# Attention with a quantised feed-forward layer on one core: SyncE's transfers by need, the exponential ahead of the rounding, the last rstd earlier

## What is computed

```python
def _L0_xattn_ref(q1, key, value, weights, bias, drop_mask):
    scores = jnp.einsum('bqd,bkd->bqk', q1, key) / 0.72
    attn = jax.nn.softmax(scores, axis=-1) * drop_mask
    o = jnp.einsum('bqk,bkd->bqd', attn, value) + bias
    return jnp.einsum('bqd,de->bqe', o, weights)

def _L0_ffn_ref(x, weight_q, weight_scale, bias):
    amax = jnp.max(jnp.abs(x2d), axis=-1, keepdims=True)
    x_scale = jnp.maximum(amax, EPS) / 127.0
    x_q = jnp.clip(jnp.round(x2d / x_scale), -128, 127).astype(jnp.int8)
    acc = jax.lax.dot_general(x_q, weight_q, (((1,), (1,)), ((), ())), preferred_element_type=jnp.int32)
    return acc.astype(jnp.float32) * x_scale * weight_scale[None, :]  (+ bias)

x = x + _L0_xattn_ref(_layernorm(x), ctx, ctx, weights, bias, mask)
x = x + _L0_ffn_ref(_layernorm(x), weight_q, weight_scale, ffn_bias)
```

## Time and profile before

| | |
|---|---|
| median of 3 runs | 329.21 us (328.72 to 329.78) |
| the profiled execution | 328.42 us, its span 326.6 us |
| TensorE matmuls | 311.9 us busy, 1418 |
| VectorE, ScalarE, GpSimd | 261.0, 240.6, 259.3 us busy |
| loads and stores | 68.39 MB, mean 209 GB/s |
| granted TensorE clock | 0.998 of full speed |

### The profile page before, as it was taken

How to read it: one execution, slowest core, us unless ns; L and a number is a source line. 1 busy time by engine, 2 the same in 40 slices (tenths; PEclk the granted TensorE clock), 3 DMA queues, 4 the chain that set the end, 5 groups by cost and what they waited for, 6 DMA issues and landing times.

```text
span 326.6 us, 5339 instructions
## 1 busy us (share of the span) xinstructions
PE 311.9 (95%) x1418; PEld 239.5 (73%) x1418; DVE 261.0 (80%) x565; ACT 240.6 (74%) x494; POOL 259.3 (79%) x362
## 2 busy tenths in 40 slices
PE   8999989999999999899998999999999999999982
PEld 7888767777777678677776777767778676776671
DVE  2998765988886899688887888788888778879775
ACT  5467867887887788788876889788787878866440
POOL 3274587897999789799997989899898879858683
PEclk9999999999999999999999999999999999999999
DMA  7995985798968979997888969998897996451112
GB/s 215 264 228 186 200 216 192 220 219 249 247 202 261 238 228 194 271 229 232 259 243 228 265 200 238 243 251 237 244 243 201 234 241 192 147 159 49 50 63 98
DMA packets 88173, 68.39 MB, mean 209 GB/s; under 512 B 25040, under 2 KB 67792, under 8 KB 88144
## 3 DMA queue, kind: packets, MB, share of 16 engines
q1 hardware_dynamic: 80368, 53.90, 65.3%
q10 hardware_dynamic: 7776, 14.16, 12.0%
HBM read 41.16 MB, written 22.54 MB: 195 GB/s over the span
## 4 chain that ended last, share of the span: by engine, by line
SPq 24%; DMA 22%; POOL 15%; ACT 11%; issue 9%; PE 9%; DVE 7%; ACTq 1%; POOLq 0%; DVEq 0%
DMA prob_rows<-probs 10%; DMA wq_rows<-prob_rows 8%; SPq L488 8%; SPq L535 7%; POOL out_tile L1526 5%; SPq L543 5%; SPq L479 4%; ACT x_round L958 2%; ACT ps_ct L1017 2%; POOL rstd L1572 2%; DVE pt_raw L1223 2%; ACT ct_hi L878 2%; ACT x_int L970 2%; POOL x_in L1560 2%; DMA norm_rows<-x_norm 1%
## 5 line engine op out<-in xcount | busy, mean ns | idle before, releaser
L636 PE MATMUL ps_attn<-vw_hi,pt_hi 128*128 128x512 f32 x120 | 47.9, 399 | 3.6 <-DVE pt_lo L1123 3.6
L636 PE MATMUL ps_scores<-ct_hi,xt_hi 128*128 128x512 f32 x124 | 48.7, 393 | 1.1 <-POOL xt_lo L1541 1.0
L638 PE MATMUL ps_scores<-ct_hi,xt_lo 128*128 128x512 f32 x124 | 48.3, 389 | 0.0
L637 PE MATMUL ps_scores<-ct_lo,xt_hi 128*128 128x512 f32 x124 | 48.3, 389 | 0.0
L638 PE MATMUL ps_attn<-vw_hi,pt_lo 128*128 128x512 f32 x120 | 46.8, 390 | 0.0
L637 PE MATMUL ps_attn<-vw_lo,pt_hi 128*128 128x512 f32 x120 | 46.8, 390 | 0.0
L1248 DVE TENSOR_TENSOR probs<-ps_scores,mask_in 128x512 f32<-128x512 f32 x32 | 22.0, 687 | 26.7 <-ACT ps_scores L981 26.3
L878 ACT ACTIVATE ct_hi<-ct_raw 128x512 fp32r<-128x512 f32 x28 | 17.7, 632 | 33.1 <-POOL out_tile L1526 30.4
L1560 POOL TENSOR_TENSOR x_in<-x_in,bias_w 128x512 f32<-128x512 f32 x32 | 41.5, 1296 | 0.7 <-issue 0.7
L1541 POOL TENSOR_TENSOR xt_lo<-xt_raw,xt_hi 128x512 fp32r<-128x512 f32 x29 | 37.7, 1301 | 4.1 <-ACT xt_hi L913 4.1
L1526 POOL TENSOR_TENSOR out_tile<-ffn_out,x_plus 128x512 f32<-128x512 f32 x28 | 39.6, 1415 | 0.0
(11 more groups left out here) (187 smaller groups left out, 820.8 us busy)
## 6 DMA issues: line engine op xcount, KB each, us to landing
x_in<-in_x_dram SPq DMA_DIRECT2D x32, 256.0 KB, 4.1
mask_in<-in_mask_BxSxS_fk_dram SPq DMA_DIRECT2D x32, 256.0 KB, 4.4
norm_rows<-x_norm ACTq DMA_DIRECT2D x30, 256.0 KB, 4.0
x_blocks<-norm_rows SPq DMA_DIRECT2D x120, 64.0 KB, 2.4
ctx_in<-in_ctx_dram SPq DMA_DIRECT2D x56, 128.0 KB, 3.9
prob_rows<-probs SPq DMA_DIRECT2D x24, 256.0 KB, 2.3
wq_rows<-prob_rows SPq DMA_DIRECT2D x96, 64.0 KB, 3.5
out_dram<-out_tile ACTq DMA_DIRECT2D x24, 256.0 KB, 4.3
```

The lines of the kernel that those rows point to most:

```text
L636: nc.tensor.matmul(bank_, lhs_hi(t), rhs_hi(t), start=(t == 0), stop=False)
L637: nc.tensor.matmul(bank_, lhs_hi(t), rhs_lo(t), start=False, stop=False)
L638: last = nc.tensor.matmul(bank_, lhs_lo(t), rhs_hi(t), start=False, stop=(t == NT - 1))
```

## The change

Four edits. On SyncE the step's order becomes: the integers, the probabilities' store, `x_blocks`, the probabilities' loads, `x_in`, the mask, and last two of the context's four issues, in every step instead of four in every second one (`load_half_pair`: in even steps the first two block rows of the pair d + 6, in odd steps the other two). On ScalarE the exponential stands ahead of `x_round` and `x_int` in the loop. On GpSimd tile 31's `inverse_deviation` stands ahead of the two additions that it followed.

```diff
--- before.py
+++ after.py
@@ -479,6 +479,17 @@
                     sp.dma_start(blocks.rearrange("i t (a c) -> i (t a) c", a=QUADS),
                                  rows[:, :, b * P:(b + 1) * P]).then_inc(loaded[k // 2], 16)
 
+            def load_half_pair(base, n, h):
+
+
+                wait_count(sp, ct_raw_ready, base, n - 4 + 2 - PER_BATCH)
+                k = slot(n, 4)
+                rows = ctx_flat[bass.ds((base + n) * P, 2 * P), :].rearrange("(a i) d -> i a d", i=BLOCK)
+                for b in range(h * QUADS // 2, (h + 1) * QUADS // 2):
+                    blocks = ctx_in[b * BLOCK:(b + 1) * BLOCK, k:k + 2, :]
+                    sp.dma_start(blocks.rearrange("i t (a c) -> i (t a) c", a=QUADS),
+                                 rows[:, :, b * P:(b + 1) * P]).then_inc(ctx_loaded[k // 2], 16)
+
             def load_rows(base, n, row):
 
                 quads = norm_rows[bass.ds(row, P), :].rearrange("(a i) d -> i a d", i=BLOCK)
@@ -551,15 +562,11 @@
             def step(base, d, row):
 
                 bounced = in_loop(base)
-                n = d + 4
-                if n % 2 == 0 and exists(base, n) and not is_tile(base, n, PER_BATCH) \
-                        and not is_tile(base, n, PER_BATCH + 2):
-
-                    wait_count(sp, ct_raw_ready, base, n - 4 + 2 - PER_BATCH)
-                    load_blocks(ctx_in, ctx_flat, row + n * P, n, 2, ctx_loaded)
                 n = d - 4
                 if exists(base, n) and (in_loop(base) or base + n < BY_PE):
                     turn_integers(base, n)
+                if bounced:
+                    store_probs(base, d - 1, row + (d - 1) * P)
                 n = d + 1
                 if is_tile(base, n, BY_PE_ROWS):
 
@@ -568,7 +575,7 @@
                 if exists(base, n) and not is_tile(base, n, 1) and (not last_batch(base) or d == 0):
                     load_rows(base, n, row + n * P)
                 if bounced:
-                    store_probs(base, d - 1, row + (d - 1) * P)
+                    load_probs(base, d - 1, row + (d - 1) * P)
                 n = d + 4
                 if exists(base, n):
 
@@ -588,8 +595,10 @@
                 if is_tile(base, d, PER_BATCH - 1):
 
                     sp.wait_ge(wq_turned, 16 * NT)
-                if bounced:
-                    load_probs(base, d - 1, row + (d - 1) * P)
+
+                n = d + 6 - d % 2
+                if exists(base, n) and base + n >= 2 * PER_BATCH:
+                    load_half_pair(base, n, d % 2)
                 n = d - 5
                 if is_tile(base, n + 1, LAST):
                     store_out(base, n, row + n * P)
@@ -1019,10 +1028,10 @@
 
                 if is_middle(base, d):
                     split_next_ctx(d + 4)
+                    exponentials()
                     if in_loop(base):
                         round_integers(d - 3)
                         store_integers(d - 3)
-                    exponentials()
                     split_next_x()
                     add_up_x(base, d + 4)
                     if in_loop(base):
@@ -1636,10 +1645,10 @@
                         add_up(d - 4)
                         add_ffn_bias(d - 2)
                     else:
+                        if is_tile(base, d - 1, LAST):
+                            inverse_deviation(d - 1)
                         add_ffn_bias(d - 2)
                         add_up(d - 4)
-                    if is_tile(base, d - 1, LAST):
-                        inverse_deviation(d - 1)
                     if is_tile(base, d - 1, LAST):
                         add_ffn_bias(d - 1)
                 if is_tile(base, d - 2, LAST):
```

## The result

The changed kernel took a median of 340.81 us in 4 runs (338.73 to 343.83), the kernel before 329.5 beside it (328.72 to 330.47). It is 11.3 us slower where 3.7 less were forecast, and lies outside the range.

A forecast was written before the change was run, and what follows sets the result against it. TensorE was taken to bound the kernel, at a floor of 9.08 us per step. Loop −2.1 and end −1.6 made −3.7 on 328.42, so 324.7; with 0.8 to the median, 325.5 us, range 321 to 330.

The forecast's parts named there:

- What bounds the kernel: TensorE, busy 311.9 of 326.6 us; 9.08 us per loop step is its floor, with 7.2 us lost above it.
- The old wait can go whole: Loop: all 7.2 us lost through the probabilities' way by HBM can go, as their store moves up past x_blocks.
- The ring through `x_in`: Loop, ScalarE's L896 round to SyncE: 14.3 us plus x_in's landing (4.4) per two steps; 9.35 per step, 5.1 lost.
- hardly a wait is left: SyncE: store needs 2.18 us before the loads back; its own 0.47 and x_blocks' 2.05 of issues cover that.
- The likeliest case: x_in lands in 4.4 us: loop −2.1, end −1.6, forecast 325.5 us; chance 0.42.
- rival 2: New wait for x_in at L896 replaces the old: landing 5.0, loop 3.9 slower, end 1.6 faster, 331.5 us; chance 0.17.
- The cause of a slow `x_in`: SyncE's x_in load, issued beside ScalarE's norm_rows store, takes turns with it: 5.0 us in one step, 4.4 assumed.
- Rival 1: No new wait: x_in lands within 3.9 us, TensorE's loop runs at 9.08 per step, 320.5 to 322 us; chance 0.28.
- The exponential at nothing: ScalarE: exponential ahead of rounding; probabilities 1.1 us earlier, integers 0.64 later, gain hidden, loss only inside the ring through x_in.
- The context at nothing: SyncE: the context's second half is issued about where its last issues were, costed at nothing.
- `x_blocks` at nothing: SyncE: x_blocks loads start 0.47 plus 0.64 us later, costed at nothing as no loop wait is for them.
- The end, −1.6: Last tile's rstd moved earlier on GpSimd: VectorE's 1.70 us wait goes, 1.6 us gained; ends 0 and −1.7.

The follow-up runs named there:

- e9_ctx_mid: Changed kernel with x_in ahead of the probabilities' loads, exponential back behind the rounding, context's two issues between x_in and those loads: 323.52 us, ratio 0.987.
- e5_sync_only: Changed kernel with the exponential put back behind the rounding on ScalarE: 339.58 us, ratio 1.038 to the kernel before.

## Why the prediction was wrong, point by point

- **What bounds the kernel**: right. TensorE's 9.08 per step is the floor, and the versions with `x_in` ahead and the exponential back reach it (9.07, and 9.10 in both runs with the last rounding moved too).
- **The old wait can go whole**: right, once nothing else stands in the way. With `x_in` ahead and the exponential back, the store's move up takes the wait for `pt_raw` from 10.5 us to 2.0 and `pt_lo` out of TensorE's waits. In the change itself it didn't, since its cause was replaced.
- **The ring through `x_in`**: right in its place and its links, wrong in the size of two terms. The step that failed is "hardly a wait is left" for the store's landing. It took the 2.18 us that the store had behind `x_blocks` for what it would have right behind the context's transfers. It landed in 3.5; the loads back start 3.59 us after the store instead of 2.5, which is 1.1 us more in the ring. The landing of `x_in` itself, taken at 4.4, has a mean of 4.7 in the loop. So the ring is 14.3 + 1.1 + 4.7 = 20.1 us, 10.05 per step (measured 10.12); with 4.7 alone it would have been 9.5 and the time near no change.
- **The likeliest case and the rivals**: the outcome has the sign and the mechanism of rival 2, at more than twice its price: against TensorE's floor the loop was to lose 11.1 us at a landing of 5.0, and it lost 232.43 − 208.8 = 23.6. None of my cases had both transfers late, so the range had no place for it.
- **The cause of a slow `x_in`**: not borne out. I put it down to ScalarE's `norm_rows` store beside it, and the Trainium skill's rule in DMA: Bandwidth & Descriptors, "Queues, rings and completion order", that engines take turns among queues, seemed to say the same. In the changed kernel the load was indeed issued within 1 us of such a store in 18 of 24 steps, but it landed in 4.6 there and in 5.3 in the other six. With `x_in` ahead of the probabilities' loads it is so in 15 of 24 steps, with 3.1 there and 3.0 elsewhere. What the profiles show instead is a pattern by what stands directly ahead on the same queue (medians in the loop): behind `x_blocks` 3.0 to 3.2, behind the probabilities' store 3.8 to 4.1, behind their loads 3.9 to 4.8, behind the mask 5.0. No run changed that neighbour alone, so the cause stays open. Rival 1 asked for 3.9 or less; that is reached behind `x_blocks`, and in the order of the change only where `x_in` is loaded a step sooner (3.9), not in the change itself (4.8).
- **The exponential at nothing**: wrong. Put into the ring it was to cost 0.64 over two steps, and there it could not be told; outside the ring, in the old order, it costs 1.9%, most likely because an issue that waits for `x_int` holds the whole of SyncE. I had said myself that SyncE's step begins with `x_int`.
- **The context at nothing, `x_blocks` at nothing**: their readers don't wait in the changed kernel, as said. But the context's transfers, moved right ahead of the store, most likely are what makes it late (2.5 with them moved away, 3.6 without): the cost lay in the queue, not at the reader.
- **The end, −1.6**: the wait went, the gain didn't come: from the last exponential to the end it is 20.9 us before and after, so this part is wrong by the prediction's own sign. I left the durations of VectorE's rounding as they were, though the edit itself puts three additions of GpSimd behind `rstd`, where the rounding runs. The trace of before had a sign of it that I did not read: of two like roundings the one beside GpSimd's last 0.43 us took 0.57 and the next 0.35.

## What to carry to other kernels

When a transfer is moved, take its landing from a place with the same neighbours ahead of it on its queue, not from its old place; and put the worst row of each landing, together, into any ring that is only a few tenths from binding. Reorder a queue that waits by what closes a loop to its next wait: here one load moved past four issues turned 3% slower into 2% faster. A wait removed at the end frees nothing if the engine that no longer is waited for then runs beside the next step and slows it; look at who will overlap with whom.

## What the runs showed of the hardware

- A VectorE `TENSOR_SCALAR` on 128x256 from SBUF takes 0.34 us (rounding) or 0.29 (integers) with no GpSimd addition beside it, and 1.31 or 1.24 beside one of 1.28 to 1.31. Each ends 0.14 to 0.16 us after the addition that it overlaps (333.53 behind 333.39, 334.81 behind 334.65), and so does the one of 0.57 in the kernel before (319.07 behind 318.93). The Trainium skill, SBUF — State Buffer, section "Who interferes with whom", says that VectorE in a two-port mode and GpSimd share a port pair that is held for a whole instruction, so that one blocks until the other is done. The trace agrees in that each ends just behind the addition, but by less than the 0.29 to 0.34 that the instruction takes alone, and no row says which mode VectorE was in. ScalarE's halves took 0.60 and 0.42, then 0.58 and 0.42, all beside additions; the Trainium skill says on the same page, in "Terms", that ScalarE has ports of its own.
- The same store of 256 KB landed in medians of 2.3, 2.5, 3.5 and 4.2 us in versions of this kernel that differ only in the order of the work on SyncE and ScalarE (before, `e9_ctx_mid`, the changed kernel, `e5_sync_only`).
- With the `rstd` edit alone, the products after the last rounding ran at a lower clock. Columns: stretch, its length, busy time and count of PE, PEld, DVE, ACT and POOL, granted clock, DMA share, GB/s:

```profile
312.69:317.20 4.51, 3.27 (x27) 2.93 (x28) 4.04 (x13) 2.87 (x5) 4.18 (x6) 1.00 0.16 58
317.20:321.50 4.30, 3.00 (x12) 1.51 (x13) 2.73 (x5) 0.77 (x2) 2.05 (x2) 0.65 0.16 61
```

A granted clock of 0.65 over the second stretch is a mix of the two levels, 1.2 and 2.4 GHz; TensorE had been idle for 1.75 us in it, waiting for the integers. The four last wide products took 1.91 us there instead of 1.03. In the changed kernel's loop the two stretches at 0.50 came 1.1 and 0.9 us after the end of idle times of 2.01 and 1.83 us at `pt_lo`. But the kernel before had idled for 1.74 at the last rounding and kept 1.00, and the run with the mask ahead had 13 idle times of up to 2.0 at `pt_lo` in its loop and kept it too. So these traces do not say what tips it. It explains why the profile of the `rstd` edit has a longer end (21.8 us from the last exponential) than the kernel before (20.9).
